# State-space layer: the expert rows reach the residual through a PSUM bank in two halves, and the statistics follow at once

## The reference

```
h = h + ffn0(layernorm(h))              # "expert rows": the rows that ffn0 wrote
x = layernorm(h)
def mamba(x):                           # run forward and on the reversed sequence
    xp, z = split(x @ W_in.T)
    xc = silu(conv4(xp) + conv_b)
    dt, Bt, Ct = split(xc @ W_xproj.T); dt = softplus(dt @ W_dt.T + b_dt)
    # 384 channels x 16 states, over 128 time steps
    state = exp(dt * A) * state + (dt * xc) * Bt
    y = sum_over_states(state * Ct) + xc * D_param
    return (y * silu(z)) @ W_out.T
h = h + 0.5 * (mamba(x) + mamba(x reversed) reversed)
```

## Time and profile before

| | |
|---|---|
| median of 3 runs | 4942.9 us (4937.89 to 4946.77) |
| the profiled execution's own time | 4934.78 us |
| its span in the trace | 4933.0 us |
| state-space layer | from about 1178 us to about 3900 us |
| one group, row addition to row addition | 166.7 to 181.4 us |
| DVE busy / PE busy over the whole span | 70% / 90% |

### The profile page before, as it was taken

The page is one execution under the profiler, slowest core; times in us unless marked ns, Lnnn a source line. Parts: engine busy times, 40 slices in busy tenths (PEclk is TensorE's granted clock), DMA queues, the critical chain, the costliest instruction groups (busy, mean ns, idle before and its releaser), DMA issues. The chain is left out here.

```text
span 4933.0 us, 62114 instructions
## 1 busy us (share of the span) xinstructions
PE 4431.2 (90%) x17128; PEld 2288.0 (46%) x17128; DVE 3453.2 (70%) x4958; ACT 2366.7 (48%) x3986; POOL 3229.0 (65%) x1657
## 2 busy tenths in 40 slices
PE   6999987996899999998989899999999877999993
PEld 4666644663334343343333344343434335666662
DVE  4766763111799999999999999999999975111114
ACT  2555542212566666665566566656566534222220
POOL 2222222441899999998989989999999932444441
PEclk9999997997999999999999999999999988999997
DMA  1000012331233233332223232323233211334335
GB/s 30 23 19 19 19 60 63 115 108 51 92 101 109 95 107 106 104 106 97 99 86 107 100 101 98 114 99 103 98 103 104 99 62 56 110 117 117 114 109 186
DMA packets 248101, 444.69 MB, mean 90 GB/s; under 512 B 37292, under 2 KB 162172, under 8 KB 247900
## 3 DMA queue, kind: packets, MB, share of 16 engines
q1 hardware_dynamic: 222556, 390.84, 24.4%
q0 software_dynamic: 25344, 51.94, 3.7%
HBM read 398.90 MB, written 43.78 MB: 90 GB/s over the span
## 5 line engine op out<-in xcount | busy, mean ns | idle before, releaser
L1688 POOL TENSOR_TENSOR m_xh<-m_u,m_Bb 128x1536 f32<-128x1536 f32 x512 | 1761.8, 3471 | 181.1 <-DVE m_u L1564 181.1
L1617 PE MATMUL bank<-m_xh,ident 128*128 128x512 f32 x3072 | 1444.6, 606 | 26.4 <-POOL m_xh L1677 26.4
L1644 ACT ACTIVATE bank<-m_dt,m_Ac 128x508 f32<-128x508 f32 x1536 | 1021.0, 683 | 474.8 <-DVE bank L1659 320.3
L1659 DVE TENSOR_TENSOR_SCAN bank<-bank,m_xh 128x512 f32<-128x512 f32 x864 | 1059.7, 1227 | 34.0 <-ACT bank L1644 7.8
L1617 PEld LDWEIGHTS bank<-m_xh,ident 128*128 128x128 f32 x3072 | 569.1, 192 | 806.3 <-issue 730.9
L1677 POOL TENSOR_TENSOR m_xh<-m_xh,m_Cb 128x1536 f32<-128x1536 f32 x224 | 773.7, 3454 | 8.8 <-DVE m_xh L1659 8.8
L1659 DVE TENSOR_TENSOR_SCAN m_xh<-bank,m_xh 128x512 f32<-128x512 f32 x672 | 771.1, 1201 | 6.6 <-POOL m_xh L1688 3.6
L1668 DVE TENSOR_TENSOR m_xh<-bank,m_Cb 128x512 f32<-128x512 f32 x864 | 597.2, 691 | 68.2 <-DMA m_Cb<-BC_rows 23.0
L1143 ACT ACTIVATE f1t_h<-bank,f1t_b 128x512 f32<-128x512 f32 x234 | 148.2, 684 | 549.6 <-PE bank L1173 549.6
L1075 POOL DMA_INDIRECT rows_y<-f1t_y,f1t_home x156 | 153.7, 985 | 338.5 <-DVE f1t_y L1113 302.9
L1478 PE MATMUL bank<-m_xp,m_dg 128*128 128x512 f32 x768 | 349.6, 597 | 3.3 <-ACT m_xc L1486 2.6
(11 more groups left out here) (333 smaller groups left out, 6217.2 us busy)
## 6 DMA issues: line engine op xcount, KB each, us to landing
m_Bb<-BC_rows SPq DMA_DIRECT2D x256, 512.0 KB, 4.7
m_Cb<-BC_rows SPq DMA_DIRECT2D x256, 512.0 KB, 3.9
f1t_w<-f_w SPq DMA_DIRECT2D x39, 576.0 KB
f1t_w1a<-f_w SPq DMA_DIRECT2D x39, 384.0 KB
f1c_yg<-rows_y SPq DMA_DIRECT2D x16, 768.0 KB, 8.3
f0t_w<-f_w SPq DMA_DIRECT2D x19, 576.0 KB
f1t_w1b<-f_w SPq DMA_DIRECT2D x78, 96.0 KB
f0t_w1a<-f_w SPq DMA_DIRECT2D x19, 384.0 KB
```

The costliest lines, as they stand in the source:

```text
L1617: mm = pe.matmul(bank[:, c, :], K.ident[:, :], xh[n % NX][:, c, :], start=False, stop=(d == 1 and n == NS - 1))
L1644: act.activation(o[:, :, lo:hi], seqs(dt[d][:, c, :])[:, :, lo:hi], ACT.Exp, scale=Ac[:, c, n:n + 1]).then_inc(s_dA, 1)
L1659: dve.tensor_tensor_scan(o, bank[:, 3 + p % 3, way], xh[n % NX][:, c, way], 0.0, ALU.mult, ALU.add).then_inc(s_h, 1)
L1688: pool.tensor_tensor(xh[n % NX][:, :, :], u[d][:, :, :], Bb[q % RB][:, n % QN, :].unsqueeze(1).to_broadcast([P, DC, TOK]), ALU.mult).then_ ...
```

## The change

ACT copies the expert rows from SBUF to the bank into which the scan writes (bank 6), two sequences (384 elements) at a time, at units 11 and 13, after the last read of states 0 to 2. DVE adds each half to `H` from PSUM at units 12 and 14, while the scans of states 3 and 4 go to `m_xh` and leave bank 6 free. ACT's second copy waits for DVE's first addition, since both halves use the same place. The statistics move from unit 22 to unit 14, behind the second addition, and POOL's part from unit 23 to 17.

```diff
-            "rows": 15, "stats": 22, "rstd": 23, "norm": 28, "pe_zT": (44, 47),
+            "act_rows": (11, 13), "rows": (12, 14), "stats": 14, "rstd": 17, "norm": 28, "pe_zT": (44, 47),
+        ROWS_IN = 3
+        s_copied = sem("rows_in_psum")
-            def dve_rows(dve):
-                hs = H[:, bass.ds(gl * G, G), :]
-                dve.wait_ge(s_got, (gl + 1) * 16)
-                dve.tensor_tensor(hs, hs, z[:, :, :], ALU.add).then_inc(s_added, 1)
+            def act_rows(act, i):
+                if i == 0:
+                    act.wait_ge(s_got, (gl + 1) * 16)
+                    if not first:
+                        stand_alone(act, K.go)
+                        act.wait_ge(s_prv, g * 2 * READS + reads(ROWS_IN))
+                else:
+                    act.wait_ge(s_added, gl * 2 + 1)
+                act.copy(bank[:, 6, 0:2 * C], z[:, 2 * i:2 * i + 2, :].rearrange("p j c -> p (j c)")).then_inc(s_copied, 1)
+
+            def dve_rows(dve, i):
+                hs = H[:, bass.ds(gl * G + 2 * i, 2), :]
+                dve.wait_ge(s_copied, gl * 2 + i + 1)
+                dve.tensor_tensor(hs, bank[:, 6, 0:2 * C].rearrange("p (j c) -> p j c", j=2), hs, ALU.add).then_inc(s_added, 1)
             def dve_stats(dve):
-                dve.wait_ge(s_added, gl + 1)
+                dve.wait_ge(s_added, gl * 2 + 2)
-                put("dve", at(POS["rows"]), dve_rows)
+                for i in two:
+                    put("act", at(POS["act_rows"][i]), act_rows, i)
+                    put("dve", at(POS["rows"][i]), dve_rows, i)
```

## The result

The changed kernel takes 4916.05 us in the median (4912.89 to 4920.03, 4 runs) beside 4944.84 us before (4937.89 to 4949.38, 4 runs); the ratio of the runs is 0.9943, with a 95% interval of 0.9926 to 0.9961. The execution that was profiled took 4920.0 us, with a span of 4918.3. Later series hold 56 more runs of the kernel before; five of them, all above 4965 us, count as slow runs and are left out of what follows.

A forecast was written before the change was run, and what follows sets the result against it. DVE sets the pace, drawing POOL and PE along. Fifteen groups +15.0, three long additions -42.6, group 0 -1.5, rows ahead of all groups +1.2: -27.9 us, from 4942.9 to 4915.0; 8 in 10 for 4896 to 4938.

The forecast's parts named there:

- The long additions: DVE's row addition at unit 15: three of 13 wait for POOL, 15.7 us each; removing them wins 3 x 14.2 us.
- the one on the other side: Rival, chance 0.07: additions with one SBUF input still queue behind POOL, nothing is saved; +36 us, 4979.
- The cover of ACT's block: Units 22 and 23: moved statistics had covered ACT's work; 1.38 us spent at unit 14, only 0.1 won.
- The decay of unit 14 behind the copy: ACT's second copy delays the gate copy and this decay; DVE stalls 0.6 us before unit 14.
- The group's sum: Net cost of an ordinary group in the state-space layer: -1.93 + 0.92 + 0.1 + 0.6 + 1.38 - 0.1 = +1.0 us.
- What was left at nothing: PE stalls about 1.4 us at later gate copies, its projection wait moves along; no loss beyond DVE's own.
- most is eaten: Rival, chance 0.13: PE's clock falls short in 15 groups, +17 us, upper-bound costs +6; about -5 us, 4938.

The follow-up runs named there:

- e4: Changed kernel without ACT's copies, both half additions reading the expert rows straight from SBUF: 4990.4 us, 1.0111 of the kernel before.
- e9: Kernel before with POOL's statistics part at unit 20 instead of 23: 4942.6 us in one execution.
- e10: Kernel before with POOL's statistics part at unit 25 instead of 23: 4987.3 us in one execution.
- e8: Kernel before, unchanged, profiled a second time: 4914.6 us with one long addition.
- e1: Changed kernel with statistics back at unit 22, POOL's part at 23, a wait for the second addition kept at unit 14: 4910.3 us, ratio 0.9943.
- e3: Changed kernel with first addition at unit 11, statistics back at unit 22 and POOL's part at 23: 4894.7 us, ratio 0.9921.
- e6: e1 with one semaphore instruction less on DVE, the statistics' own wait left out: 4897.2 us, ratio 0.9942.
- e7: e3 with one semaphore instruction less on DVE, the statistics' own wait left out: 4899.7 us, ratio 0.9939.
- e2: Changed kernel with the first addition at unit 11 instead of 12: 4911.8 us, ratio 0.9965.

## Why the prediction was right, and where it was not

**The time**: 4915.0 forecast, 4916.05 measured; 28.8 us less than before, against 27.9. The cause is shown. The closeness is largely luck, since the median of four runs of the kernel before depends on how many long additions they hold: in the two later series its median is 4930 us, 14 us above 4916 and not 29.

**The long additions** (-42.6 us in the sum): shown, by the changed profile, where the largest addition is 0.56 us, by e4, where the SBUF source brings them back, and by e9 and e10, which set their length. The Trainium skill's SBUF — State Buffer, section "SBUF: two separate sides", has the shared pair held for the whole instruction by whichever starts first. The prediction read this as a wait for one POOL operation at most, 4.4 us with the addition; no long addition fits that reading, at 12.1, 15.7 and 19.0 us: the waiting DVE operation can lose several times in a row. The Trainium skill's same page, section "Who interferes with whom", says that a DVE instruction with at most one SBUF input, outside the 2-port modes, does not contend with GpSimd; the 0.53 us of the additions from PSUM beside a busy POOL agree.

Rival "the one on the other side" is out: all 32 additions with one SBUF input took 0.53 to 0.56 us.

The weak step is that I took three as the number of long additions in a run; the profiles of the kernel before have three, one and three. Profile against profile the change won only 14.8 us (4934.8 to 4920.0), and e8 shows the kernel before at 4914.6 us, faster than the changed one's median of 4916.

**The cover of ACT's block**: shown. Wait before unit 23 1.18 us, forecast 1.3; with the statistics back it goes (e1, e3, e6, e7).

**The decay of unit 14 behind the copy**: shown. 0.53 us, forecast 0.6; the copy took 0.48 us as worked out; with the first addition at unit 11 the wait goes (e2).

**The group's sum**: +1.0 forecast, about +1.4 us measured. From the scan of unit 12 to that of unit 16 the changed group takes 8.76 us (to 2475.90) and that of the earlier trace rows 7.37, +1.39 instead of the +1.07 of the sum's terms for this stretch; and the means of the windows at full clock, 168.4 and 166.9 us, differ by 1.5. The terms that were too small are the handovers: 0.67 us from the second addition to the statistics where I had 0.56, and 1.57 us from the statistics to the scan behind them where I had 1.38. Why these are longer was not tested.

**What was left at nothing**: PE's clock. In the earlier trace rows a fall costs 1.1 us; the new idle stretch on PE (1.3 us, 1.4 foreseen) was put down as no loss. In the windows of the changed kernel two falls together go with up to 6 us (174.25 against 168.15), and two windows are above the 170 us that the prediction named as the sign of the clock or PE. What the change itself does to the clock isn't shown: the changed kernel has 9 falls and 37.5 us at one half, the kernel before, long additions left out, 7, 9 and 13 falls and 23.9 to 44.4 us in its three profiles.

**The sums together**: in the 13 windows of the first profile the change won 18.3 us. Three long additions give -42.6 and 13 groups at +1.4 give +18.2; the 6 us that are left are about what half of the 13.6 us more at one half clock would cost. Against kernels with no long addition, the rest of the change costs 4916 - 4897 = about 19 us, where my terms give 14.7 and the same terms with +1.4 a group 20.7. So the size that was off is the group's sum. Rival "most is eaten" (the clock) has no share that can be told from the spread between profiles of one kernel.

## What to carry to other kernels

An instruction's mean far above its minimum (5166 beside 959 ns) is a reason to look at each of its rows: three outliers in thirteen were the whole gain here. An operation of VectorE with two SBUF inputs beside a GpSimd that is never idle took twice its bare 0.96 us as a rule and up to 15.7 us; with one of the inputs in PSUM each half took 0.53 us. Before moving work away from a place where nobody waits, look which engine ends just in time there; 0.15 us of margin said that 1.38 us of work on DVE were cover for ACT. When runs of one kernel spread, compare profiles stage by stage, and take more than one of each. When an edit adds an instruction to a hardware loop, read the first instructions behind the branch before giving the time to the edit.

## What the runs showed of the hardware that was not expected

- One instruction more in DVE's loop (406 instead of 405 in this program) made the way from the branch to the next instruction 3.6 instead of 2.9 us in every round. Whether it is the number or the place of the loop in memory was not told apart.
- PE's clock fell to one half in stretches of mostly 3.4 us, 5 to 22 times in thirteen windows, and of 13.7 us behind each long addition, after PE had been idle for 13.5 us. The number of the short ones doesn't go with the total of PE's waits in any way that I found: e3 and e6 had 5, e7 14 and 13. This is open.
- How many additions of the kernel before are held up until POOL has nothing to do varies from execution to execution, three, one and three in its profiles, at 14.2 us each.
